# Channel mixes as straight code over sequences, with the store inside the last, and row statistics moved into the stages ahead

## The reference

```python
def _layernorm(x, axis=-1, eps=1e-05):
    m = jnp.mean(x, axis=axis, keepdims=True)
    v = jnp.var(x, axis=axis, keepdims=True)
    return (x - m) / jnp.sqrt(v + eps)

# the channel mix, of layers 5 and 7; x is the layernorm here
x_prev = jnp.concatenate([jnp.zeros((B, 1, C), x.dtype), x[:, :-1, :]], axis=1)
xr = mu_r * x + (1.0 - mu_r) * x_prev
xk = mu_k * x + (1.0 - mu_k) * x_prev
r = jax.nn.sigmoid(jnp.einsum('btc,dc->btd', xr, W_r))
k = jnp.einsum('btc,dc->btd', xk, W_k)
k_act = jnp.square(jax.nn.relu(k))
out = r * jnp.einsum('btc,dc->btd', k_act, W_v)
```

## Time and profile before

| what | value |
| --- | --- |
| median of 3 runs | 5688.43 us (5683.7 to 5716.82) |
| the profiled execution | 5650.74 us, its span 5649.0 us |
| TensorE busy | 4205.9 us, 74% of the span |
| VectorE, ScalarE, GpSimd busy | 3119.3, 2358.3, 1804.7 us |
| attention, layer 0 (38 to 1035 us) | 997 us, TensorE busy 771.78 |
| banded attention, layer 2 (1509 to 2562) | 1053 us, TensorE busy 953.23 |
| each mixture, layers 1 and 3 | 436 us, TensorE busy 227.54 and 228.48 |
| each channel mix, layers 5 and 7 | 146 us, TensorE busy 86.63 and 86.41 |
| BN_STATS of one statistics stage | 12.46 us, ahead of 4.32 us of BN_AGGR |

### The profile page before, as it was taken

One profiled execution on the slowest core, in us unless ns is written; L12 is line 12 of the kernel. 1 busy time (PEld: TensorE's weight loads), 2 busy tenths in 40 slices (PEclk: granted clock), 3 DMA queues, 4 the chain that ended last, 5 costly groups with the idle time before them and its releaser, 6 DMA issues. The chain is left out here.

```text
span 5649.0 us, 187383 instructions
## 1 busy us (share of the span) xinstructions
PE 4205.9 (74%) x73124; PEld 2512.6 (44%) x73126; DVE 3119.3 (55%) x7536; ACT 2358.3 (42%) x4503; POOL 1804.7 (32%) x2618
## 2 busy tenths in 40 slices
PE   3888788539189999994571999999657799995645
PEld 1333333338045555553560233333246688882224
DVE  4555555434356666654333777777456555407864
ACT  0444444225045555541340566666535433214433
POOL 2333333140555555541314222232012233204431
PEclk9798878669599999995785899999867799997767
DMA  2111111211100000001111111111001211260001
GB/s 65 41 44 42 43 39 35 66 50 52 36 2 3 2 2 2 2 2 38 51 53 40 46 41 46 41 44 43 3 4 63 79 44 38 58 199 23 22 13 30
DMA packets 252868, 218.42 MB, mean 39 GB/s; under 512 B 63619, under 2 KB 221252, under 8 KB 252486
## 3 DMA queue, kind: packets, MB, share of 16 engines
q1 hardware_dynamic: 244294, 196.20, 11.3%
q0 software_dynamic: 8192, 16.79, 1.0%
HBM read 139.24 MB, written 73.14 MB: 38 GB/s over the span
## 5 line engine op out<-in xcount | busy, mean ns | idle before, releaser
L691 DVE TENSOR_REDUCE l_M<-l_max_bank 128x1 f32<-128x512 f32 (+3 forms) x2048 | 1100.8, 584 | 683.2 <-PE l_max_bank L494 428.9
L650 ACT ACTIVATE l_probs<-l_exp_bank 128x1024 f32<-128x1024 f32 (+3 forms) x1024 | 876.4, 865 | 784.7 <-PE l_exp_bank L509 750.5
L488 PE MATMUL l_max_bank<-l_KS,l_QS 48*128 48x512 bf16 (+3 forms) x2048 | 644.3, 374 | 214.0 <-DVE l_M L691 153.8
L473 PE MATMUL l_out_bank<-l_probs,l_V 128*32 128x256 f32 (+2 forms) x6144 | 548.3, 437 | 28.3 <-ACT l_heads_out L608 16.5
L509 PE MATMUL l_exp_bank<-l_QS,l_KS 49*128 49x512 bf16 (+3 forms) x2048 | 471.5, 366 | 13.8 <-ACT l_probs L650 13.7
L488 PEld LDWEIGHTS l_max_bank<-l_KS,l_QS 48*128 48x128 bf16 x2048 | 166.0, 96 | 682.9 <-DVE l_M L691 565.2
L390 POOL TENSOR_SCALAR_AFFINE_SELECT l_probs<-l_probs 128x256 f32<-128x256 f32 x512 | 207.0, 408 | 606.1 <-ACT l_probs L650 596.8
L1809 DVE TENSOR_REDUCE l_M<-l_max_bank 128x4 f32<-128x512 f32 x256 | 175.4, 686 | 170.0 <-PE l_max_bank L1628 170.0
L874 POOL DMA_INDIRECT l_back<-main_sorted_out,l_index x128 | 121.9, 952 | 413.3 <-issue 413.3
L431 POOL TENSOR_TENSOR l_qk<-l_qk,l_cos 128x512 f32<-128x512 f32 x32 | 40.6, 1270 | 602.6 <-ACT l_rot L626 602.6
L1469 POOL TENSOR_TENSOR l_rms<-l_rms,l_minus_half 128x20 f32<-128x20 f32 x64 | 226.1, 3532 | 12.4 <-POOL l_rms L1466 12.4
(11 more groups left out here) (417 smaller groups left out, 10348.6 us busy)
## 6 DMA issues: line engine op xcount, KB each, us to landing
l_parts_dram<-l_parts SPq DMA_DIRECT2D x64, 384.0 KB, 2.5
l_fir_band<-in_dr_short_dram SPq DMA_DIRECT2D x16, 1024.0 KB, 5.6
l_fir_band<-in_dr_long_dram SPq DMA_DIRECT2D x16, 1024.0 KB, 8.0
l_QS<-l_parts_dram SPq DMA_DIRECT2D x128, 96.0 KB
l_KS<-l_parts_dram SPq DMA_DIRECT2D x128, 96.0 KB
l_kqv_dram<-l_in_out SPq DMA_DIRECT2D x16, 768.0 KB, 3.5
l_core_ring<-l_kqv_dram SPq DMA_DIRECT2D x48, 256.0 KB, 3.4
l_rows<-main_sorted_in SPq DMA_DIRECT2D x152, 64.0 KB, 1.8
```

The costliest lines, as they stand in the source:

```text
L473: last = nc.tensor.matmul(out_bank[STRIP * h:STRIP * (h + 1), q0:q1], V[:, par, kb, 4 * j + h, :], probs[:, 2 * kb + h // 2, h % 2, q0:q1] ...
L488: return nc.tensor.matmul(max_bank[:, g, 0:W[t]], QS[64 * g:64 * g + ROWS, to, i, t * P:(t + 1) * P], KS[64 * g:64 * g + ROWS, to, i, 0:W[ ...
L650: nc.scalar.activation(probs[:, n, :, Q0[kb]:T], exp_bank[:, u % 2, :, Q0[kb]:T], ACT.Exp, scale=float(D) ** -0.5).then_inc(exp_done, 1)
L691: nc.vector.reduce_max(M[:, j % 2, col:col + 1], max_bank[:, g, 0:W[t]], AX.X)\
```

## The change

1. `channel_mix` is written out over the 16 sequences instead of looping over pairs, and each engine's order is shifted. TensorE: turns 0 and 1, then for each b: k and r of b, turn of b+2, values of b-1. VectorE: mixes of b+1, normalise b+3, product and add of b-1. ScalarE as before, with the copy of b+2 last, and a Sigmoid of one column at the start. The waits are those of two buffers, from the third sequence on. TensorE turns the first two sequences before it waits for the weights.
2. In layer 7 SyncE stores two sequences at a time as soon as they are added (eight transfers of 512 KB); the stage `store_x` is left out.
3. `halves` lives for the whole program. The BN_STATS are issued where X was written last: in `load_x` (each group of four sequences on its own semaphore), at the end of each sequence in the mixture's last loop, and once per tile in banded attention. The statistics stages of layers 0, 2, 3 and 4 only aggregate; those of layers 1, 5, 6 and 7 are as before.

```diff
+def token_sums(vector, X, halves, tiles):
+    for t in range(TPS):
+        vector.bn_stats(halves[:, tiles, :][:, t, :], X[:, tiles, :][:, t, :])
...
 def load_x
...
-                             io["x"][b:b + 4].rearrange("b (t p) c -> p (b t) c", p=P)).then_inc(loaded, 16)
-            sp.wait_ge(loaded, 64)
+                             io["x"][b:b + 4].rearrange("b (t p) c -> p (b t) c", p=P)).then_inc(loaded[b // 4], 16)
+            for n in range(B // 4):
+                sp.wait_ge(loaded[n], 16)
...
+            for b in range(B):
+                dve.wait_ge(loaded[b // 4], 16)
+                token_sums(nc.vector, X, halves, slice(b * TPS, (b + 1) * TPS))
...
 def mixture, the last loop
...
                     place_of(b + 2, n)
+                    dve.wait_ge(added, b + 3)
+                    token_sums(v, X, halves, bass.ds(b * TPS, TPS))
...
 def channel_mix
...
+            if out is not None:
+                for b in range(0, B, 2):
+                    sp.wait_ge(added, b + 2)
+                    sp.dma_start(out[b:b + 2].rearrange("b (t p) c -> p (b t) c", p=P),
+                                 X[:, b * TPS:(b + 2) * TPS, :]).then_inc(stored, 16)
+                sp.wait_ge(stored, 16 * (B // 2))
...
+            turn(0)
+            turn(1)
             pe.wait_ge(loaded, LOADED)
-            pe.wait_ge(hn_ready, 1)
-            turn(0)
-            with pe.Fori(0, B // 2) as i:
...
+            for b in range(B):
+                project(b)
+                if b + 2 < B:
+                    turn(b + 2)
+                if b:
+                    values(b - 1)
+            values(B - 1)
...
+            act.wait_ge(made, 2)
+            nc.scalar.activation(one[:, :], one[:, :], ACT.Sigmoid)
+            keep_hT(0)
+            keep_hT(1)
...
+            mixes(0)
+            normalise(2)
+            for b in range(B):
+                if b + 1 < B:
+                    mixes(b + 1)
+                if b + 3 < B:
+                    normalise(b + 3)
+                if b:
+                    add(b - 1)
+            add(B - 1)
...
 def window_attention, VectorE
...
+                def sums_of_rows(k, t):
+                    bank, n = bank_of(b, "OUT", k, t), b.at(TPS, TPS * k + t)
+                    dve.wait_ge(misc_free[bank], turns_before(b, "OUT", k, t) + 1)
+                    v.bn_stats(tile_of(halves, n), tile_of(X, n))
...
                         maxima(*reduce_of, 0)
+                    if out_of is not None:
+                        sums_of_rows(*out_of)
```

More of the change, by code:

```diff
@@ L723, in tile_of, with mixture @@
     return x[:, bass.ds(tile, 1), :].rearrange("p o c -> p (o c)")
-def mixture(nc, tag, io, X, stats, identity, sorted_in, sorted_out, first):
+def mixture(nc, tag, io, X, halves, stats, identity, sorted_in, sorted_out, first):
     with Stage(nc, tag) as s:
@@ new lines, in project @@
+            def project(b):
+                n = b % 2
+                pe.wait_ge(mixed, b + 1)
+                if b >= 2:
+                    pe.wait_ge(relu_done, b - 1)
+                nc.tensor.matmul(k_bank[:, n, :], w["k"][:, :], mix[:, n, 0, :], start=True, stop=True)\
+                  .then_inc(k_done, 1)
+                if b >= 2:
+                    pe.wait_ge(gate_ready, b - 1)
+                for t in range(TPS):
+                    last = nc.tensor.matmul(r_bank[:, n, t * P:(t + 1) * P], mix[:, n, 1, t * P:(t + 1) * P],
+                                            w["r"][:, :], start=True, stop=True)
+                last.then_inc(r_done, 1)
@@ new lines, in values @@
+            def values(b):
+                n = b % 2
+                pe.wait_ge(squares_ready, b + 1)
+                if b >= 2:
+                    pe.wait_ge(product_ready, b - 1)
+                for t in range(TPS):
+                    last = nc.tensor.matmul(y_bank[:, n, t * P:(t + 1) * P], squared[:, n, t * P:(t + 1) * P],
+                                            w["v"][:, :], start=True, stop=True)
+                last.then_inc(y_done, 1)
+            turn(0)
+            turn(1)
@@ L1249, in _, with normalise @@
         @block.vector
         def _(dve):
-            dve.sem_inc(mixed, 2)
-            dve.sem_inc(added, 2)
-            def normalise(b, n):
-                tokens, moments = X[:, bass.ds(b * TPS, TPS), :], stats[:, bass.ds(b * TPS, TPS), :]
+            def normalise(b):
+                n = b % 2
+                if b >= 2:
+                    dve.wait_ge(turned, b - 1)
+                tokens, moments = X[:, b * TPS:(b + 1) * TPS, :], stats[:, b * TPS:(b + 1) * TPS, :]
                 for t in range(TPS):
@@ L1259, in normalise @@
                 last.then_inc(hn_ready, 1)
-            normalise(0, 0)
-            dve.wait_ge(loaded, LOADED)
-            with dve.Fori(0, B // 2) as i:
-                for n in range(2):
-                    b = i * 2 + n
-                    dve.wait_ge(diff_ready, b + 1)
-                    dve.wait_ge(r_done, b + 1)
-                    for j in range(2):
-                        last = nc.vector.scalar_tensor_tensor(mix[:, n, j, :], diff[:, n, :], mu[:, j:j + 1],
-                                                              hT[:, n, 0:T], ALU.mult, ALU.add)
-                    last.then_inc(mixed, 1)
-                    dve.wait_ge(turned, b + 1)
-                    normalise(b + 1, (n + 1) % 2)
-                    dve.wait_ge(y_done, b + 3)
-                    dve.wait_ge(gate_ready, b + 3)
-                    nc.vector.tensor_tensor(product[:, n, :], gate[:, n, :], y_bank[:, n, :], ALU.mult)\
-                      .then_inc(product_ready, 1)
-                    dve.wait_ge(product_ready, b + 1)
-                    x = X[:, bass.ds(b * TPS, TPS), :].rearrange("p t c -> p (t c)")
-                    nc.vector.tensor_tensor(x, x, product[:, n, :], ALU.add).then_inc(added, 1)
@@ new lines, in mixes, with add @@
+            def mixes(b):
+                n = b % 2
+                dve.wait_ge(diff_ready, b + 1)
+                if b >= 2:
+                    dve.wait_ge(r_done, b - 1)
+                for j in range(2):
+                    last = nc.vector.scalar_tensor_tensor(mix[:, n, j, :], diff[:, n, :], mu[:, j:j + 1],
+                                                          hT[:, n, 0:T], ALU.mult, ALU.add)
+                last.then_inc(mixed, 1)
+            def add(b):
+                n = b % 2
+                dve.wait_ge(y_done, b + 1)
+                dve.wait_ge(gate_ready, b + 1)
+                nc.vector.tensor_tensor(product[:, n, :], gate[:, n, :], y_bank[:, n, :], ALU.mult)\
+                  .then_inc(product_ready, 1)
+                dve.wait_ge(product_ready, b + 1)
+                x = X[:, b * TPS:(b + 1) * TPS, :].rearrange("p t c -> p (t c)")
+                nc.vector.tensor_tensor(x, x, product[:, n, :], ALU.add).then_inc(added, 1)
@@ L1288 @@
+            normalise(0)
+            normalise(1)
+            dve.wait_ge(loaded, LOADED)
+            mixes(0)
+            normalise(2)
+            for b in range(B):
+                if b + 1 < B:
[5 more added lines that the diff above has]
+            add(B - 1)
 QH, KVH, HD, WINDOW = 16, 4, 64, 64
```

135 lines of the change are left out of this document (60 added, 75 removed).

## The result

The changed kernel takes **5502.76 us**, median of 4 runs (5482.32 to 5513.03), against 5686.66 for the kernel before (4 runs, 5683.7 to 5716.82). The ratio is 0.966, with a 95% interval of 0.962 to 0.970: 184 us less. The forecast was 5504. The sum hit, but one of its terms was too small by a factor of six, and errors in the others made up for it.

What follows compares the result with a forecast made beforehand. Channel mixes were held bound by TensorE and VectorE taking turns, with serial row statistics and a store tail besides. 126.4 + 45.0 + 13.3 - 0.5 = 184 us off the 5688.43 median gives 5504 us, range 5475 to 5560.

Steps and rivals of the forecast that it cites:

- Period of the channel mix: Layers 5 and 7: time per sequence falls from 8.59 to 4.6 us, between 4.1 and 6.2.
- the rival in which TensorE stays at the lower level: Channel mixes: TensorE at the lower clock is full at 6.2 us a sequence, 48 us worse, 5552; chance 0.10.
- The collision: Channel mix: GpSimd's subtraction lengthens VectorE's work by up to 0.51 us a sequence, 3.85 to 4.36 at worst, 4.2 taken.
- Head and tail: Channel mix: first k 2.5 us sooner, and 6.5 us instead of 7.4 after the last k.
- Channel mixes together: Layers 5 and 7: 63.2 us less in layer 7, the same code in layer 5, 126.4 us in all.
- Pipeline opens: Channel mix: sequences overlap; the rival that a wait keeps the period at 8.6 us gives 5626, chance 0.04.
- Statistics, load: Load stage: transfers land one after the other, so only the last 16 BN_STATS are exposed, 3.1 us.
- Statistics, removed pieces: Statistics stages of layers 0, 2, 3 and 4: each drops its 12.47 us of BN_STATS, 49.9 us.
- Statistics in banded attention: Layer 2: one BN_STATS per tile fits VectorE's 1.01 us idle before the reciprocal, costing nothing; 19 us without that cover.
- Statistics in the mixture: Last loop of layers 1 and 3: four BN_STATS fit the gather wait; 0.9 us exposed per layer, 1.8 in all.
- Store: End of layer 7: 4.9 us instead of 18.3 follow the last add, saving 13.3 us.
- Slower by fetch of code: Straight channel mix: code fetch stalls TensorE every sequence; 5.8 us each cancels the gain, 7.5 gives 5744; chance 0.03.

Runs made afterwards that it cites:

- scalar_normalise: Changed kernel with the channel mix's four normalises per sequence moved from VectorE to ScalarE; 5504.19 us, ratio 0.967.
- the first trace: Profiled execution of the unaltered kernel before, from which the prediction read its waits; 5650.74 us around a span of 5649.0.
- the second execution of before: The kernel before, unaltered, run once more for its trace; 5684.51 us.
- store_stage: Changed kernel with the old separate store stage behind the new channel mix instead of the eight transfers inside layer 7; 5529.42 us, ratio 0.972.
- old_order: Changed kernel with the channel mix still written out and one table load, but each engine in the old order; 5624.76 us, ratio 0.988.
- both: Changed kernel with VectorE's scatter and gather loops of the mixture as straight code and the channel mix's normalise on ScalarE; 5468.22 us, ratio 0.962.

## Why the prediction was right, step by step

- **Period of the channel mix**: forecast 4.6 us from two loads of 4.2 each and an allowance for unevenness; measured 4.30, within 4.1 to 6.2. The mechanism held, VectorE as the fuller engine: in `scalar_normalise` the period falls to 3.75 once its load is taken off. The parts were less right than the sum. VectorE's own work was put at 3.85 us and is 3.67, the interval without a collision, because back to back the normalise costs 1.03 us and the add 0.61. The collisions were put at 0.35 us a sequence; they are 9.5 us in layer 5 and 8.5 in layer 7, 0.5 to 0.6 for each of 16 sequences and 0.79 where the clock is full. These two errors cancel in part, and that is luck. The last sequences, which have nothing to normalise, pull the mean down further. TensorE was less of a rival than assumed, with a clock of 0.90 instead of 0.86.
- **Clock**: the rival in which TensorE stays at the lower level (chance 0.10) fell. The granted clock was 0.90 with TensorE busy 84%, between the rows of 0.85 and 1.00 from which it was read the earlier trace rows.
- **The collision**: forecast at up to 0.51 us of a VectorE instruction, called half of the subtraction's 1.04. That misread: the add began 0.39 us after the subtraction, so only 0.65 were left of it, and 0.51 is most of that. Where the overlap was longer so was the loss: 0.78 for the normalises, 0.79 for the mixes, 0.79 for the add in `scalar_normalise`. The rule of the Trainium skill (SBUF — State Buffer, "Who interferes with whom"), a lock for the whole instruction, describes these instances better than my 0.51; the same section counts the normalise's kind, with one tensor read from SBUF, among those that can collide in a two-port mode (no run here shows in which mode it ran). Its price of 4.9 us a sequence did not come: the period was 4.30, and 4.46 where the clock was full, because VectorE's own work was shorter than 3.85, each collision cost 0.2 to 0.3 us less than the subtraction lasts, and 3 to 5 of the 16 subtractions of a stage lengthened nothing.
- **Head and tail**: first k 1.9 us sooner after the start of the stage (forecast 2.5), 5.7 us from the last k to the end of the last add (6.5).
- **Channel mixes together**: forecast 126.4 us. Layer 5 fell by 68.1 from the first trace and 65.2 from the second one; for layer 7 `store_stage` gives 67.3 and 64.4. That is 130 to 135, 3 to 9 more than forecast, most of it the period (30 x 0.3 = 9).
- **Pipeline opens**: the rival that it doesn't (0.04) fell. `old_order` has 5625 us, where the prediction said 5626, but that it fits to 1 us is chance: its period is 8.05 and not 8.6, some 16 us less for both layers, and the mixtures' loss is in it.
- **Statistics, load**: forecast 3.1 us for the last group; the stage grew by 3.3 to 3.6. The transfers landed one after the other.
- **Statistics, removed pieces**: 49.9 forecast, 52.4 measured, since loop and semaphores of each stage went too.
- **Statistics in banded attention**: forecast nothing; the layer took 1055.0 us in the changed kernel and 1053.6 to 1056.8 in the others that carry the sums, and 1052.6 to 1054.6 in the three that don't. The cover held to within 2 us; the idle time before the reciprocals fell from 90.2 to 77.6 us in all.
- **Statistics in the mixture: this step was wrong.** The term was 0.9 us per mixture, only the last sequence exposed. It is 5.5 to 6 us, or 11 instead of 1.8 for both. The failing thought is "Four BN_STATS (0.8 us) fit". They do, in 2.8 us of idle time, in most sequences. But I counted VectorE's work and not the register instructions and the stalls around it, and the earlier trace rows came from an execution that had neither. How this loss arises is partly shown. In the looped form the sums' register instructions of 0.70 us delay the index copy that GpSimd waits for. In straight code with the sums the loop is 5 to 8 us longer than in the one execution without, by one or two stalls of some 5 us, in which VectorE and GpSimd stand together. Why the chip does either remains open; the runs only show both beside indirect transfers, and the second kind only where the sums were.
- **Store**: forecast 13.3 us; 13.7 by `store_stage`. From the last add to the end it is 5.3 us (forecast 4.9).
- **Slower by fetch of code** (0.03): fell. The straight channel mixes and the straight mixture loops are the faster ones, and between the first and the last k of layer 7 TensorE never stands for more than 1.9 us, where this case needs 5.8 each time.
- **The base.** The same terms gave 5504 from the median of before and 5467 from the profiled execution, and 5504 was right. The measured terms add up, from the second execution of before, to 143.3 for channel mixes and store, 52.4 for the removed pieces, less 3.6 in load and 10.8 in the gather loops: 181 us. (The two traces themselves lie 171 us apart, since layers 0, 4 and 6 and the scatter loops, which the change leaves alone, differ too.) The gain in the mix and in the removed pieces made up for the loss in the mixtures. That these errors cancelled is luck; that the first trace was 38 us below the median was visible and should have made me distrust each wait read from it in a loop that I meant to fill.

## What to carry to other kernels

Where two engines take turns, look for the wait in each direction; here shifting one of them by a whole sequence with the buffers already there brought 3.75 of 4.29 us, and afterwards the load of the fuller engine, collisions included, was the period. Add up that load from start to start of instructions that follow without a break, and price a collision by how much of the other instruction is left when yours begins. An idle time is cover only for what it covers in every execution: count the address arithmetic with the work, and try straight code in short loops beside indirect transfers (here 81 us instead of 85 to 90 in the scatter). When a profile lies outside the runs' spread, take the sum from the median and a second profile before believing a small term.

## What the runs showed of the hardware

- Register and branch instructions of VectorE that take 0.04 to 0.10 us took 0.70 in stretches of up to some 20 us: 50 to 72 times in each of the nine other executions with register loops, never in the first trace of before. They lie beside GpSimd's indirect transfers. The written-out loops had none (in `both`, three fell into the loop over the experts, which still has registers).
- In the straight gather loops with the sums VectorE and GpSimd stood still together five times in four loops, VectorE for 4.7 to 5.9 us and GpSimd for 3.4 to 4.8, with no packet on the instruction queues. No run here tells why.
- Where GpSimd's subtraction (1.03 us) met VectorE's normalises, mixes or add in full, these took 0.78 to 0.79 us longer; where only 0.65 us of it were left, 0.51. In steady operation such collisions made every other sequence 5.24 us long instead of 3.67.
- The granted clock was 0.72 in the stretch with TensorE busy 86.41 of 146 us, 0.90 with 53.54 of 64, 0.96 with 52.12 of 56. It isn't fixed by the instructions alone: layer 0, with the same ones everywhere, got 0.82 to 0.87 from one execution to the next.
- Layer 0 took 996 to 1030 us between executions; differences under some 10 us in the total had to be read from the stages.
